# Cross attention on one core: keys projected behind the scores, values behind the output, context split between the query scalings

## The reference

```
q = xn @ Wq + bq            # 16 heads of 128, each scaled by its root mean square
k = ctx @ Wk + bk           # 4 heads of 128, likewise
v = ctx @ Wv + bv           # 4 heads of 128
p = softmax(q k^T / sqrt(128) + mask)     # 64 x 64 for each head; 4 query heads share a key head
x = x + (p @ v) @ Wo
```

## Time and profile before

| | |
|---|---|
| median of three runs | 1478.65 us (1475.2 to 1479.37) |
| the profiled execution, its own time | 1476.5 us |
| its span in the trace | 1474.7 us |
| mean granted TensorE clock | 0.94 |
| busy share of the span: PE, PEld, DVE, ACT, POOL | 87%, 70%, 68%, 49%, 26% |
| the sublayer of the change | from about 749 to 1171 us |

### The profile page before, as it was taken

How to read it: one execution, slowest core, us unless ns; L and a number is a source line. 1 busy time by engine, 2 the same in 40 slices (tenths; PEclk the granted TensorE clock), 3 DMA queues, 4 the chain that set the end, 5 groups by cost and what they waited for, 6 DMA issues and landing times. The chain is left out here.

```text
span 1474.7 us, 27997 instructions
## 1 busy us (share of the span) xinstructions
PE 1282.2 (87%) x9980; PEld 1038.4 (70%) x9996; DVE 1001.1 (68%) x1882; ACT 720.4 (49%) x1492; POOL 388.0 (26%) x482
## 2 busy tenths in 40 slices
PE   4888887199999985799968999999998699999998
PEld 3666665055565554478946777878786599999998
DVE  4767776267777745589855877777786557655555
ACT  1555555157777773440035555555656245333332
POOL 1112120344444310248654212121212021112210
PEclk9999999579999997579988999999999699999999
DMA  3000000345454400200040000000000110010001
GB/s 107 1 0 0 0 0 1 80 119 130 105 134 117 114 19 7 96 1 0 0 130 8 4 7 4 7 4 7 4 6 1 41 46 23 22 37 30 2 1 58
DMA packets 49003, 54.31 MB, mean 37 GB/s; under 512 B 7365, under 2 KB 44837, under 8 KB 46245
## 3 DMA queue, kind: packets, MB, share of 16 engines
q1 hardware_dynamic: 48936, 53.41, 13.0%
HBM read 42.52 MB, written 10.49 MB: 36 GB/s over the span
## 5 line engine op out<-in xcount | busy, mean ns | idle before, releaser
L677 DVE TENSOR_REDUCE fa_neg_max<-psum 128x2 f32<-128x512 f32 x256 | 167.9, 689 | 58.1 <-PE psum L854 57.2
L738 ACT ACTIVATE fa_probs<-psum 128x1024 f32<-128x1024 f32 x128 | 130.3, 1018 | 39.1 <-PE psum L865 35.4
L1627 PE MATMUL psum<-mo_xT_high,mo_w_high 128*128 128x256 f32 x512 | 145.4, 284 | 3.5 <-DVE mo_w_low L2286 3.5
L1627 PE MATMUL psum<-mo_xT_low,mo_w_high 128*128 128x256 f32 x512 | 145.0, 283 | 0.0
L1627 PE MATMUL psum<-mo_xT_high,mo_w_low 128*128 128x256 f32 x512 | 144.3, 282 | 0.0
L854 PE MATMUL psum<-fa_k_stack,fa_q_stack 72*128 72x256 bf16 x512 | 104.1, 288 | 35.6 <-DMA fa_k_stack<-k_parts 33.9
L2241 ACT ACTIVATE mo_silu<-psum 128x256 f32<-128x256 f32 x128 | 49.1, 384 | 159.3 <-PE psum L1627 159.3
L1748 POOL TENSOR_TENSOR ga_q_scaled<-ga_q,ga_q_inv 128x1024 f32<-128x1024 f32 x32 | 63.4, 1984 | 216.0 <-ACT ga_q_inv L1789 216.0
L2375 DVE TENSOR_TENSOR mo_mid<-mo_silu,psum 128x256 f32<-128x256 f32 x128 | 53.7, 420 | 96.0 <-ACT mo_silu L2241 95.9
L1627 PEld LDWEIGHTS psum<-mo_xT_high,mo_w_high 128*128 128x128 f32 x512 | 97.2, 190 | 3.9 <-DVE mo_w_low L2286 3.9
L1627 PEld LDWEIGHTS psum<-mo_xT_low,mo_w_high 128*128 128x128 f32 x512 | 97.2, 190 | 0.0
(11 more groups left out here) (405 smaller groups left out, 3613.3 us busy)
## 6 DMA issues: line engine op xcount, KB each, us to landing
fa_q_stack<-q_parts SPq DMA_DIRECT2D x16, 576.0 KB
fa_k_stack<-k_parts SPq DMA_DIRECT2D x16, 576.0 KB
k_parts<-fa_parts SPq DMA_DIRECT2D x80, 64.0 KB, 2.6
q_parts<-fa_parts SPq DMA_DIRECT2D x48, 64.0 KB, 5.2
x<-in_x SPq DMA_DIRECT2D x4, 512.0 KB, 5.6
fa_context<-in_ctx SPq DMA_DIRECT2D x16, 128.0 KB, 2.1
staged<-in_ga_w_q SPq DMA_DIRECT2D x1, 2048.0 KB, 9.6
ga_ctxT<-in_ctxT SPq DMA_DIRECT2D x16, 128.0 KB, 2.2
```

The lines of the kernel that those rows point to most:

```text
L677: nc.vector.tensor_reduce(neg_max[:, b, :, h], ps[:, h % 2, :].rearrange("p (q k) -> p q k", q=2), AX.X, ALU.max, negate=True).then_inc(ma ...
L738: nc.scalar.activation(probs[:, g].rearrange("p h k q -> p h (k q)"), ps[:, 2 + 2 * (g % 2):4 + 2 * (g % 2), :], ACT.Exp).then_inc(exp_don ...
L1627: done = nc.tensor.matmul(out, lhsT[i], rhs[j], start=start and k == 0, stop=stop and k == 2)
```

## The change

It moves instructions and adds none. TensorE does the keys of tile t+1 right behind the scores of tile t, then the mix of t-1, then query pieces one to three; the values go behind the output, ahead of the transposes of the keys. VectorE does the keys' bias and their sum of squares first in the turn. ScalarE squares the keys behind the scores and makes their inverse norm between the second and third high part of the mix; all four query squares now stand ahead of the exponential. The split of the context rows is done for tile t+2 late in the turn in place of t+1 early in it: ScalarE's part behind the first inverse norm of the queries, GpSimd's part between the two halves of `scale_queries`. SP's loads become a plain loop. The shift by the maximum stays where it is, on VectorE. The first context rows are split in turn -2.

```diff
-            def turn(t, valid):
-                if valid(t + 2) and started(t, -1):
-                    sp.wait_ge(ctx_lows, t + 2)
-                    sp.dma_start(ctxT[:], ctx_rows[:, :, bass.ts(t + 2, P)]).then_inc(ctx_ready, 16)
-
-            pipeline(sp, turn)
+            with sp.Fori(1, TILES) as n:
+                sp.wait_ge(ctx_lows, n)
+                sp.dma_start(ctxT[:], ctx_rows[:, :, bass.ts(n, P)]).then_inc(ctx_ready, 16)
...
+            def context_low(n):
+                pool.wait_ge(ctx_highs, n + 1)
+                nc.gpsimd.tensor_tensor(ctxT_low[:], ctxT[:], ctxT_high[:].bitcast(F32), ALU.subtract).then_inc(ctx_lows, 1)
...
-                if valid(t + 1):
-                    pool.wait_ge(ctx_highs, t + 2)
-                    nc.gpsimd.tensor_tensor(ctxT_low[:], ctxT[:], ctxT_high[:].bitcast(F32), ALU.subtract).then_inc(ctx_lows, 1)
+                if isinstance(t, int) and t == -2:
+                    context_low(0)
...
                 if valid(t + 1):
                     scale_queries(0)
+                if valid(t + 2) and started(t, -1):
+                    context_low(t + 2)
+                if valid(t + 1):
                     scale_queries(1)
...
+            def context_high(n):
+                act.wait_ge(ctx_ready, 16 * n + 16)
+                if started(n, 1):
+                    act.wait_ge(v_psum, n)
+                nc.scalar.copy(ctxT_high[:], ctxT[:]).then_inc(ctx_highs, 1)
...
-                if valid(t + 1):
-                    square(t + 1, 0)
-                if valid(t - 1):
-                    for j in range(G_KV):
-                        take_mixed(t - 1, j)
+                if valid(t - 1):
+                    take_mixed(t - 1, 0)
+                    take_mixed(t - 1, 1)
+                if valid(t + 1):
+                    act.wait_ge(k_sums, t + 2)
+                    nc.scalar.activation(k_log[:], k_sum[:], ACT.Ln, bias=rms_eps[:], scale=1.0 / G_HD).then_inc(k_logs, 1)
+                    act.wait_ge(k_logs, t + 2)
+                    nc.scalar.activation(k_inv[:], k_log[:], ACT.Exp, scale=-0.5).then_inc(k_invs, 1)
+                if valid(t - 1):
+                    take_mixed(t - 1, 2)
+                    take_mixed(t - 1, 3)
...
                 if valid(t + 1):
-                    square(t + 1, 1)
-                    square(t + 1, 2)
+                    for g in range(4):
+                        square(t + 1, g)
...
                     query_rms(t + 1, 0)
+                if valid(t + 2) and started(t, -1):
+                    context_high(t + 2)
...
                 if valid(t + 1):
+                    dve.wait_ge(k_psum, t + 2)
+                    nc.vector.tensor_tensor(k_raw[:], ps[:, 2, :], bias_k[:], ALU.add).then_inc(k_ready, 1)
+                    dve.wait_ge(k_squared, t + 2)
+                    nc.vector.tensor_reduce(k_sum[:], k_squares[:].rearrange("p (j d) -> p j d", d=G_HD), AX.X, ALU.add).then_inc(k_sums, 1)
                     biased(t + 1, 0)
...
                 if valid(t + 1):
-                    pe.wait_ge(xT_ready, t + 2)
-                    query(t + 1, 0)
+                    if isinstance(t, int) and t == -1:
+                        pe.wait_ge(w_k_split, KC)
+                    pe.wait_ge(ctx_lows, t + 2)
+                    key_or_value(2, w_k_high, w_k_low, k_psum)
...
                 if valid(t + 1):
-                    query(t + 1, 1)
-                    query(t + 1, 2)
+                    pe.wait_ge(xT_ready, t + 2)
+                    for g in range(3):
+                        query(t + 1, g)
...
                 if valid(t + 1):
                     if isinstance(t, int) and t == -1:
                         pe.wait_ge(loaded, LOADS)
+                        pe.wait_ge(w_v_split, KC)
+                    if started(t, 0):
+                        pe.wait_ge(v_lows, t + 1)
+                    key_or_value(3, w_v_high, w_v_low, v_psum)
                     pe.wait_ge(k_ready, t + 2)
```

More of the change, by code:

```diff
@@ L1809, in turn @@
                     done.then_inc(scoresT_ready, 1)
+                if isinstance(t, int) and t == -2:
+                    context_high(0)
                 if valid(t + 1):
-                    act.wait_ge(ctx_ready, 16 * t + 32)
-                    if started(t, 0):
-                        act.wait_ge(v_psum, t + 1)
-                    nc.scalar.copy(ctxT_high[:], ctxT[:]).then_inc(ctx_highs, 1)
+                    act.wait_ge(k_ready, t + 2)
+                    nc.scalar.activation(k_squares[:], k_raw[:], ACT.Square).then_inc(k_squared, 1)
                 if isinstance(t, int) and t == -1:
@@ L1834, in turn @@
                 if valid(t + 1):
-                    act.wait_ge(k_ready, t + 2)
-                    nc.scalar.activation(k_squares[:], k_raw[:], ACT.Square).then_inc(k_squared, 1)
-                    square(t + 1, 3)
                     query_rms(t + 1, 0)
+                if valid(t + 2) and started(t, -1):
+                    context_high(t + 2)
+                if valid(t + 1):
                     act.wait_ge(kT_psum, t + 2)
@@ L1853, in turn @@
                     take_queries(t + 1, 3)
-                    act.wait_ge(k_sums, t + 2)
-                    nc.scalar.activation(k_log[:], k_sum[:], ACT.Ln, bias=rms_eps[:], scale=1.0 / G_HD).then_inc(k_logs, 1)
-                    act.wait_ge(k_logs, t + 2)
-                    nc.scalar.activation(k_inv[:], k_log[:], ACT.Exp, scale=-0.5).then_inc(k_invs, 1)
             pipeline(act, turn)
@@ L1916, in turn @@
                 if valid(t + 1):
-                    dve.wait_ge(k_psum, t + 2)
-                    nc.vector.tensor_tensor(k_raw[:], ps[:, 2, :], bias_k[:], ALU.add).then_inc(k_ready, 1)
                     biased(t + 1, 3)
@@ L1940, in turn @@
                     nc.vector.tensor_tensor(xT_low[:], ps[:, 7, 0:E], xT_high[:].bitcast(F32), ALU.subtract).then_inc(xT_ready, 1)
-                if valid(t + 1):
-                    dve.wait_ge(k_squared, t + 2)
-                    nc.vector.tensor_reduce(k_sum[:], k_squares[:].rearrange("p (j d) -> p j d", d=G_HD), AX.X, ALU.add).then_inc(k_sums, 1)
                 if isinstance(t, int) and t == -1:
@@ L2033, in turn @@
                     query(t + 1, 3)
-                    if isinstance(t, int) and t == -1:
-                        pe.wait_ge(w_k_split, KC)
-                        pe.wait_ge(w_v_split, KC)
-                    pe.wait_ge(ctx_lows, t + 2)
-                    key_or_value(2, w_k_high, w_k_low, k_psum)
-                    if started(t, 0):
-                        pe.wait_ge(v_lows, t + 1)
-                    key_or_value(3, w_v_high, w_v_low, v_psum)
                 if valid(t):
```

## The result

| | before | after |
|---|---|---|
| median on one chip | 1479.01 us (4 runs, 1475.2 to 1483.37) | 1500.08 us (4 runs, 1499.4 to 1501.68) |
| ratio, 95% interval | | 1.0133 (1.0109 to 1.0156) |
| span of the profiled execution | 1474.7 us | 1499.9 us |
| the sublayer in it | 748.8 to 1172.3: 423.5 us | 753.7 to 1196.5: 442.8 us |
| one turn of the loop, mean of 13 | 24.00 us | 25.34 us |

The forecast was 1500.3 us in a range of 1484.5 to 1506. The turns of the loop are counted from the scores of tile 1 to those of tile 14, here and in all that follows: 799.10 to 1111.14 before, 808.19 to 1137.66 after.

What follows compares the result with a forecast made beforehand. The loop was taken to be bound by a chain through TensorE, VectorE, GpSimd and TensorE. 17.8 (turns 1 to 13) + 0.8 + 1.0 + 2.1 gave +21.7 us, 1476.5 to 1498.2, or 1500.3 for the median; range 1484.5 to 1506.

Steps and rivals of the forecast that it cites:

- The chain: Loop turn: TensorE up to the transposed scores, VectorE's queue, GpSimd, then TensorE's last transposes and next scores set the period.
- Part 1: TensorE's order: keys' matmuls ahead of the mix bring the transposed scores 1.40 us later; values behind the output cost nothing.
- Part 2: VectorE's queue: keys' bias leaves the run, 0.60 us less; first sum of squares moves by +1.40 - 0.60 = +0.80 us.
- Part 3: ScalarE: moved key norm and context split, exponential behind the fourth square; covered by 0.5 us or more, costs nothing.
- turn 0: First turn, before the loop's turns 1 to 13: +1.5 us by the same steps, partly taken up by TensorE's slow clock: +1.0.
- Part 4: GpSimd's queue: context's low half between the scalings; +1.37 us a turn with the multiply's hold, +0.41 with plain queueing.
- the hold: VectorE's multiply holds GpSimd's low half until 1.08 us after the multiply's start, so the second scaling ends at +7.37.
- The rival without a hold: In the loop the low half only queues: 13 x 0.41 = 5.3, total +8.6 us, 1487.3; chance 12%.
- The pauses: TensorE's waits ahead of the two halves of the query transposes grow to 1.0 and 1.4 us.
- the two things forecast: Turn -1: TensorE starts at 758.3, not 755.70, waiting for GpSimd's splits, 1.4 us; low half meets VectorE's cast, 0.7 us.
- if GpSimd got in first: Between the scalings, low half ahead of the multiply: multiply holds second scaling until 5.45; +1.35 us or a little less.
- the 2.15 us that I added for the median: The shown median, 1478.65, lay 2.15 us above the profiled execution, so forecast 1498.2 became 1500.3 us.

Runs made afterwards that it cites:

- keys twice: Changed kernel with the keys' six matmuls done twice, ahead of the mix: 1519.05 us, 26.51 us a turn.
- the last two kernels: Mixed split and second norm early, on the kernel before: 1470.28 us; on the changed kernel, also exponential earlier, low half behind both scalings: 1471.95 us.
- the first six experiments: Low half last 1487.9, keys' bias back 1510.43, no multiply 1482.29, keys twice 1519.05, values twice 1505.46 on changed kernel; context part alone on before 1485.24 us.

## Why the prediction was right, step by step

**The chain.** Right for the kernels before and after: it was forecast that the turn follows TensorE up to the transposed scores, then VectorE, then GpSimd. Each part was moved by itself: +1.17 for work in the first (keys twice), +0.59 in the second, +0.69 and +1.00 in the third. In the last two kernels of the experiments the first link is another one: there VectorE's run from the mix's low parts on sets when the mask starts.

**Part 1, +1.40.** Measured 9.58 - 8.15 = +1.43. The values' new place cost nothing, as said; the run with them twice shows how much more it would bear.

**Part 2, -0.60.** Measured 7.37 - 7.96 = -0.59, so +0.84 at the first sum of squares for +0.80.

**Part 3, nothing.** Right in the loop. The exponential is issued at 976.30 and ends at 977.34; the sum over it is due when the first sum of squares is done, at 978.33. The cover was 1.0 us; I had said 0.5 or more. ScalarE's exponential and VectorE's sum over it:

```profile
976.30 1.04 ACT L1848 ACTIVATE ga_probs<-ga_probs 128x1024 f32<-128x1024 f32 x1
```

```profile
978.33 1.21 DVE L1940 TENSOR_REDUCE ga_total<-ga_probs 128x16 f32<-128x1024 f32 x1
```

It failed in turn 0, below.

**Part 4, +1.37 with the hold.** Counted from the first sum of squares (951.86), the second scaling was forecast to end at 7.37 and ends at 959.19, so at 7.33. The loop's 13 turns took 17.4 us more for 17.8. The rival without a hold asked for a low half of 0.74 us and turns of 24.4; the rows show 1.75 and 25.34. On the rule of the Trainium skill, page "SBUF — State Buffer", section "Who interferes with whom" (a VectorE instruction with two SBUF inputs and a GpSimd instruction share a pair, held by the first to issue): the trace agrees in all of these runs, and the run without the multiply shows which instruction it is. That it is the second SBUF input that matters, no run varied by itself. The rows fit it, though: VectorE's second sum of squares, with one input, runs beside the first scaling in every turn, and both take their usual time.

```profile
979.07 1.90 POOL L1749 TENSOR_TENSOR ga_q_scaled<-ga_q,ga_q_inv 128x1024 f32<-128x1024 f32 x1 [19.89 <-ACT ga_q_inv L1792]
```

```profile
979.46 1.21 DVE L1888 TENSOR_REDUCE ga_q_sum<-ga_q_scaled 128x8 f32<-128x1024 f32 x1
```

By that page of the Trainium skill the first to issue holds the pair for its whole instruction. Each of these rows gives 1.08 of the multiply's 1.22 us, and the measured figure decides: the sum went by it.

**The pauses.** Forecast at 1.0 and 1.4 us, measured 0.75 and 1.35. The first was 0.25 too long, and most of it is the output's wait for the mask, which I had put at under 0.1 us. TensorE's last query matmul and first output matmul:

```profile
971.87 0.40 PE L1627 MATMUL psum<-w_q_low,ga_xT_high 128*128 128x512 f32 x1
972.27 0.38 PE L2057 MATMUL psum<-ga_w_o_high,ga_mixedT_high 128*128 128x256 f32 x1
```

These matmuls follow each other at 0.23 us (six in 1.40), so the output could start at 972.10; the mask ends at 970.91 + 1.23 = 972.14, and it starts at 972.27, 0.17 late. From the transposed scores to the keys' transposes TensorE takes 9.61 us (979.45 - 969.84) where 10.75 less 1.40 was due: these are the 0.26 us from above. They cost nothing, as said: the later pause takes them up, and is shorter by as much.

**The sum, and luck.** Over the whole sublayer the single terms were off and made up for each other:

| stretch | forecast | before | after | measured |
|---|---|---|---|---|
| sublayer's start to the scores of tile 0 | +2.1 | 27.95 | 29.42 | +1.5 |
| turn 0 | +1.0 | 22.34 | 25.06 | +2.7 |
| turns 1 to 13 | +17.8 | 312.04 | 329.47 | +17.4 |
| turn 14 | +0.8 | 23.91 | 24.71 | +0.8 |
| scores of tile 15 to the end | 0 | 37.27 | 34.09 | -3.2 |
| sum | +21.7 | 423.5 | 442.8 | +19.2 |

For the stretch ahead of turn 0 I can say that the two things forecast are there: TensorE's first matmul of the keys comes 8.8 us behind the sublayer's start (9.5 forecast), and the low half beside VectorE's cast takes 2.77 us at 776.44. The sum of the two was 0.6 too high.

In turn 0 the step that failed is the +1.40 of Part 1. The transposed scores came at 9.85 us behind the scores (792.98 - 783.13) and not at 6.94 + 1.40, so +2.9. TensorE ran at the lower of its two clock levels for longer; its scores and the next matmul, before and after, and the clock (last figure but two) while it did the scores:

```profile
776.76 2.73 PE L2007 MATMUL psum<-ga_qT,ga_kT 128*64 128x256 f32 x16
779.42 0.50 PE L1627 MATMUL psum<-w_q_high,ga_xT_high 128*128 128x512 f32 x1
```

```profile
776.76:779.42 2.66, 2.66 (x18) 1.42 (x17) 0.00 (x0) 0.99 (x3) 0.48 (x1) 0.69 0.00 0
```

```profile
783.13 3.68 PE L2017 MATMUL psum<-ga_qT,ga_kT 128*64 128x256 f32 x16
786.74 0.80 PE L1627 MATMUL psum<-ga_w_k_high,ga_ctxT_high 128*128 128x512 f32 x1
```

```profile
783.13:786.74 3.61, 3.61 (x17) 1.72 (x16) 0.00 (x0) 0.59 (x1) 0.45 (x1) 0.50 0.00 0
```

The scores cost 0.95 us more by it, the keys' matmuls take 1.82 us in place of 1.40, and a pause of 0.15 us stands ahead of the third query piece. TensorE had waited 3.20 us for GpSimd just before, where it was 2.49; that this kept the clock down is not shown. The other steps of turn 0 held: the first sum of squares moved by -0.59 against the transposed scores, the second scaling by +0.98 against that sum (I had some 0.7), and TensorE's own transposes at the lower clock took up 0.58 of it, where I had put 0.5. The order of the hold turned round:

```profile
800.50 1.22 DVE L1940 TENSOR_REDUCE ga_total<-ga_probs 128x16 f32<-128x1024 f32 x1 [0.52 <-ACT ga_probs L1848]
...
803.04 1.60 DVE L1947 TENSOR_TENSOR ga_probs<-ga_probs,ga_inv 128x1024 f32<-128x1024 f32 x1
```

```profile
802.84 0.72 POOL L1742 TENSOR_TENSOR ga_ctxT_low<-ga_ctxT,ga_ctxT_high 128x256 fp32r<-128x256 f32 x1
803.52 2.88 POOL L1749 TENSOR_TENSOR ga_q_scaled<-ga_q,ga_q_inv 128x1024 f32<-128x1024 f32 x1
```

The sum waited 0.52 us for the exponential. In turn 0 there is no mix of a tile before, so the 1.57 us of its low parts are missing from VectorE's run, and with them the cover of 1.0 us: Part 3 was worked out for the loop alone. So the multiply came 0.20 us behind the low half in place of ahead of it. The low half took its usual 0.72, the multiply 1.60, and the scaling 2.88. This is the case "if GpSimd got in first", and its end fits the figures of that step too: the multiply went on from 804.64 - 1.22 = 803.42, plus 1.08 plus 1.90 is 806.40, the scaling's end.

The last row of the table, two turns without any keys, queries or values, was forecast to stay. It is shorter by 3.2 us, and I see no part of the change in it (ScalarE's two instructions less are the keys' inverse norm of tile 15, now ahead of the scores): busy time from the scores of tile 15 to the sublayer's end, before and after.

```profile
1135.05:1172.32 37.27, 25.26 (x177) 23.13 (x176) 16.95 (x30) 10.27 (x20) 0.00 (x0) 0.77 0.00 1
```

```profile
1162.37:1196.46 34.09, 21.50 (x177) 19.36 (x176) 16.95 (x30) 9.78 (x18) 0.00 (x0) 0.90 0.00 1
```

The same 177 matmuls took 25.26 us at a mean clock of 0.77 and 21.50 at 0.90. So the clock was the step left out here, and the sublayer's +19.2 in this pair of profiles is +22.4 with the tail left out, for +21.7.

Outside the sublayer the profiles differ by 4.9 us ahead of it and 1.0 behind it. That code is the same in both and no part of the change. With it the profiled execution took 1501.68 us, where 1498.2 was forecast; the 2.15 us that I added for the median then hid most of that. The medians' difference of 21.1 us rests on four runs each, which scatter over 8.2 us before and 2.3 after. The agreement in the loop, 17.4 for 17.8, is what the runs bear out; the agreement of the whole to 0.2 us is chance.

## What to carry to other kernels

Ask of a small instruction not only how long it takes but beside what it will be issued. GpSimd's 0.74 us stood behind 5.01 us of idle time at the head of the turn; 0.06 us behind VectorE's multiply of two SBUF operands it cost 0.69 us a turn more than behind the second scaling. Where the bound is a chain through several engines, measure it in its links (scores to transposed scores, to the first sum, to the last scaling): in the first six experiments each edit showed in one link, to a few hundredths of a microsecond, where the whole time scatters by several. Look each time whether the link still ends what is waited for: in the last two kernels the mask no longer waited for the transposed scores, and the two links on either side of them traded 1.7 us that meant nothing. And give work that the chain doesn't need the place where the chain's engine waits anyway.

## What the runs showed of the hardware that I had not expected

- **The tail's clock.** The last two turns, in which TensorE has long waits, took from 33.2 us at a mean clock of 0.95 (keys twice) to 37.3 at 0.77 (before). Over the ten profiles, in order of the clock: 0.77 37.27 (before), 0.81 35.87, 36.00, 35.74, 35.92, 36.35, 0.85 34.83, 0.90 34.09 (after) and 33.97, 0.95 33.23. Most of these kernels differ in nothing there; those that do (no multiply, the last two kernels) lie in line. TensorE's busy time for the same 177 matmuls goes from 20.68 to 25.26 us. So the tail moves by up to 4 us with the clock, as much as several terms of this prediction. Why the clock differs from one execution to the next stays open.
- **Who comes first can turn round in one kernel.** The low half and the multiply are issued 0.06 us apart in the loop and 0.20 us the other way in turn 0. Both ends follow from the same figures (1.08 us from when the multiply gets its turn, then each instruction's own time), but in turn 0 part of the cost shows on VectorE.
- **A held instruction is measured by what is left of the hold.** Beside the same multiply the same low half shows 1.75 us (issued 0.06 us behind its start) and 1.07 (with the values twice), and the same scaling 2.21, 2.52 and 2.88. So here the duration in a row of GpSimd is not the price of its work.
- **The stages ahead scatter.** The sublayer began between 748.7 and 754.2 us in the ten profiles, though nothing ahead of it was changed; that spread of 5.5 us is in every comparison of single whole times above.
